# Linear attention of a decoder layer: values as the stationary operand, denominators in every lane

## The chip, the cores and the metric

The kernel runs on one core of a Trainium2 chip. The metric is the device time of the core in microseconds (us), taken over several executions; the median counts.

## The reference

One decoder layer in three parts, each followed by a layer norm over the sum with its input: causal linear attention with a feed-forward (the first layer), cross-attention to a context of 375 rows (the second), and a feed-forward with 8 experts (the third). Only the first layer's attention is touched:

```python
q = _phi((h @ wq).reshape(b, s, H, DH), proj)      # phi(x) = elu(x @ proj) + 1
k = _phi((h @ wk).reshape(b, s, H, DH), proj)
v = (h @ wv).reshape(b, s, H, DH)
# for each t, over the keys up to t:
kv = kv + k_t[..., :, None] * v_t[..., None, :]
ksum = ksum + k_t
num = einsum('bhd,bhde->bhe', q_t, kv)
den = einsum('bhd,bhd->bh', q_t, ksum) + 1e-06
out_t = num / den[..., None]
attn = out.reshape(b, s, H * DH) @ wo
```

There are 32 sequences of 112 rows, 256 columns wide, with H = 16 heads of DH = 64.

## The kernel before

The first layer works on 8 groups of 4 sequences: the first and the last are written out, the six between are a loop (`groups`, L222). All f32 weights and activations of the projections are split into a high and a low f16 part, and a product is three f16 products (`split_product`, L59). The scores and values of the attention are plain f32 products.

Inside a group the attention is worked in 16 units of four heads of one sequence (`unit`, L156); units 2n and 2n+1 are a pair, whose scores are computed together: even heads use array rows 0 to 63, odd heads rows 64 to 127. The order of the work is written out by hand: each engine has a `body(g)` that walks through 24 steps t, and issues what is due at that step. A unit passes these stations:

- `scores` (TensorE, L299): keys as weights, queries streamed, so that keys lie in the lanes: 112 keys x 112 queries per head, in one PSUM bank per half.
- `take_scores` (ScalarE, L439) copies the bank of a unit to one of four buffers `sm`; `mask` (GpSimd, L659) sets the entries above the diagonal to zero. Row 112 of `sm` holds 1e-6.
- `values` (TensorE, L312), two steps later: the scores of a head are the weights (112 columns), and 65 columns of `v1` are streamed, 64 of v and one of ones. Queries lie in the lanes of the result, and its 65th column is the denominator.
- `divide` (VectorE, L527), a step later: a reciprocal of 4 denominators per lane and a multiply of 256 columns into `o32`. Two PSUM banks `o_ps` alternate: values of unit u wait for the division of unit u-2.
- `turn_output` (TensorE, L321), once per pair: four turns through the identity bring the outputs to inner dimension in the lanes, in a bank of the shared pool `pb` of four.
- `out_high` (ScalarE, L429) and `out_low` (VectorE, L540) split the turned outputs into f16 parts.
- `rows_out` (TensorE, L328): the output projection with `wo`, once per sequence (four units), 24 products of 256 columns; it waits for the low halves.

Between these, the bodies place work of the neighbours: layer-norm statistics and rows of this group, the last and the next, the turn of the next group's normed rows (t = 15), its first two query tiles (t = 20), on VectorE the residual sums (L591). After the 24 steps come the rest of the next group's query, key and value projections, the turn of the second norm, the feed-forward with GELU, and its output rows; there `phi` (ScalarE L404, VectorE L518) and `take_v` (ScalarE, L421) follow TensorE. The pool `pb` is handed out in one fixed order of uses (`attention_uses`, L177; `MAIN`, L190), each waiting for the use four before.

Of the kernel before, what the change touches and what calls it, by code (L numbers as in the profile page):

```python
# [98 lines left out]
def layer1(nc, a, x_sb, ident, half_neg, consts_done, passed, sb_in, psum_in, sem):  # L99
# [7 lines left out]
    with stack:  # L107
# [24 lines left out]
        v1 = sb("v1", [P, G4, H, DH + 1], F32)  # L132
        sm = sb("sm", [P, NSM, 4 * T], F32)
        rec = sb("rec", [T, 2, 4], F32)
        o32 = sb("o32", [T, 2, 8 * DH], F32)
# [41 lines left out]
        def attention_uses(last):  # L177
            uses = []
            for t in range(STEPS):
                if TURN_AT <= t < UNITS + TURN_AT and (t - TURN_AT) % 2 == 1:  # L180
                    uses.append(("O", (t - TURN_AT) // 2))
                if t == T1_AT and not last:
                    uses += several("T1", KD)
                if t == Q_AT and not last:
                    uses += several("Q", EARLY)
                if t >= W_AT and (t - W_AT) % 4 == 0:
                    uses.append(("W", (t - W_AT) // 4))
            return uses
# [33 lines left out]
        def groups(eng, body):  # L222
# [13 lines left out]
        s_ready, s_copied, s_masked, av_done, rec_done, o_done, o_hi_done = (  # L236
            sem(f"a_{n}") for n in ("s_ready", "s_copied", "s_masked", "av_done", "rec_done", "o_done", "o_hi_done"))
# [16 lines left out]
        def _(pe):  # L254
# [57 lines left out]
            def values(g, u):  # L312
                b, heads = unit(u)
                pe.wait_ge(s_masked, UNITS * g + u + 1)
                at_least(pe, o_done, UNITS * g + u - 1)
                for i, h in enumerate(heads):
                    mm = pe.matmul(o_ps[u % 2][0:T, i * (DH + 1):(i + 1) * (DH + 1)], sm[0:T + 1, u % NSM, i * T:(i + 1) * T],
                                   v1[0:T + 1, b, h, :], start=True, stop=True)
                mm.then_inc(av_done, 1)

            def turn_output(g, j):  # L321
                pe.wait_ge(o_done, UNITS * g + 2 * j + 2)
                ps = claim(use(g, "O", j))
# [10 lines left out]
            def body(g):  # L334
                written(g, "V", 2 * G4)
                for t in range(STEPS):
# [4 lines left out]
                    if TURN_AT <= t < UNITS + TURN_AT and (t - TURN_AT) % 2 == 1:  # L341
                        turn_output(g, (t - TURN_AT) // 2)
# [43 lines left out]
        def _(act):  # L386
# [34 lines left out]
            def take_v(g, pieces):  # L421
                for i in pieces:
# [3 lines left out]
                    act.activation(v1[0:T, b, 8 * n:8 * n + 8, 0:DH], bank(u)[0:T, :].rearrange("p (h d) -> p h d", d=DH),  # L426
                                   ACT.Identity, scale=UNSCALE).then_inc(free_of(u), 1)

            def out_high(g, j):  # L429

                b, half = divmod(j, 2)
                u = use(g, "O", j)
                act.wait_ge(pb_ready, ready(u))
# [60 lines left out]
        def _(dve):  # L494
# [32 lines left out]
            def divide(g, u):  # L527

                ps = o_ps[u % 2][0:T, 0:4 * (DH + 1)].rearrange("p (i d) -> p i d", d=DH + 1)
                dve.wait_ge(av_done, UNITS * g + u + 1)  # L530
                at_least(dve, o_done, UNITS * g + u - 1)
                dve.reciprocal(rec[:, u % 2, :], ps[:, :, DH]).then_inc(rec_done, 1)
                dve.wait_ge(rec_done, UNITS * g + u + 1)
                if u >= 4:
                    dve.wait_ge(pb_ready, ready(use(g, "O", u // 2 - 2)))
                dst = o32[:, u // 2 % 2, :].rearrange("p (i r d) -> p r i d", r=2, d=DH)[:, u % 2, :, :]
                dve.tensor_tensor(dst, ps[:, :, 0:DH],
                                  rec[:, u % 2, :].unsqueeze(2).to_broadcast([T, 4, DH]), ALU.mult).then_inc(o_done, 1)

            def out_low(g, j):  # L540
                b, half = divmod(j, 2)
                u = use(g, "O", j)
# [109 lines left out]
        def _(pool):  # L652
# [28 lines left out]
            pool.memset(v1[:, :, :, 0:DH], 0.0).then_inc(pads_done, 1)  # L681
            pool.memset(v1[:, :, :, DH], 1.0).then_inc(pads_done, 1)
# [1379 lines left out]
```

## Time and profile before

| what | us |
|---|---|
| median of 3 runs | 2336.74 (2332.95 to 2337.68) |
| the profiled execution, its own time | 2328.24 |
| its span | 2326.5 |
| TensorE (PE) busy | 2204.5 (95%) |
| weight loads (PEld) busy, beside PE | 1646.4 (71%) |
| VectorE (DVE) busy | 1529.9 (66%) |
| ScalarE (ACT) busy | 1386.3 (60%) |
| GpSimd (POOL) busy | 763.1 (33%) |

The first layer fills the span up to about 750 us. A busy share is an average over stages. Matmul records overlap: one lasts longer than the step from its start to the next one's, so costs on TensorE are read from starts. An f32 product of scores or values stands as two records.

### The profile page before, as it was taken

What the parts mean: (1) busy time and instruction counts of PE and PEld (TensorE: products, weight loads), DVE (VectorE), ACT (ScalarE), POOL (GpSimd) and SP (SyncE); (2) the same over time, 40 slices, a digit from 0 to 9 for tenths busy, and PEclk for the clock granted to TensorE, in tenths of its full rate; (3) what the DMA queues carried; (4) which work ended last, traced back from release to release, by engine and by line L of the source; (5) the groups of instructions that cost most, each with busy time, mean ns of one, the idle gap of its engine ahead of it and who ended that gap; (6) DMA issues with size and microseconds to landing.
All of it is one profiled execution on the core that took longest, in us unless ns stands there. A gap on an engine that the chain in (4) does not pass through costs nothing. (4 is left out here: it accounts for less than half of the span.)

```text
span 2326.5 us, 57836 instructions
## 1 busy us (share of the span) xinstructions
PE 2204.5 (95%) x20778; PEld 1646.4 (71%) x20778; DVE 1529.9 (66%) x4387; ACT 1386.3 (60%) x3169; POOL 763.1 (33%) x1335
## 2 busy tenths in 40 slices
PE   5999999999997599999999999999999999989997
PEld 3776876876875366777677777767777767768886
DVE  4555455555544477777777777777777777566657
ACT  4556456456452367676767676776767676644534
POOL 1121221221211345444444444444445454200003
PEclk8999999999999699999999999999999999879999
DMA  5100000000000300000000000000000000042202
GB/s 137 39 2 1 0 0 0 0 0 0 0 1 1 102 10 16 10 16 11 15 14 12 16 10 15 10 16 10 16 10 15 10 9 2 1 109 91 92 1 64
DMA packets 45732, 51.44 MB, mean 22 GB/s; under 512 B 19120, under 2 KB 37664, under 8 KB 45504
## 3 DMA queue, kind: packets, MB, share of 16 engines
q1 hardware_dynamic: 45504, 48.45, 7.1%
q8 instruction: 137, 2.24, 0.4%
q14 instruction: 91, 0.75, 0.1%
HBM read 44.78 MB, written 3.67 MB: 21 GB/s over the span
## 5 line engine op out<-in xcount | busy, mean ns | idle before, releaser
L1450 POOL TENSOR_SCALAR p_norm<-p,p_rec 112x375 f32<-112x375 f32 x512 | 304.3, 596 | 630.5 <-DVE p_rec L1301 540.9
L1305 DVE TENSOR_TENSOR pt_lo<-b_t,pt_hi 125x336 f16<-125x336 f32 x512 | 258.0, 504 | 164.4 <-ACT pt_hi L1180 163.2
L1287 DVE CUSTOM_DVE_ANT_0 s_neg<-b_s,mask_bias 112x375 f32<-112x375 f32 x512 | 274.8, 537 | 95.6 <-PE b_s L1021 88.9
L1180 ACT ACTIVATE pt_hi<-b_t 125x336 f16<-125x336 f32 x512 | 227.6, 445 | 138.1 <-PE b_t L1030 136.2
L1174 ACT ACTIVATE p<-s_neg,neg_max 112x375 f32<-112x375 f32 x512 | 307.9, 601 | 0.5 <-DVE neg_max L1287 0.5
L1030 PE MATMUL b_t<-ident,p_norm 112*125 112x112 f32 x1536 | 274.2, 288 | 9.0 <-POOL p_norm L1450 2.5
L1030 PEld LDWEIGHTS b_t<-ident,p_norm 112*125 112x125 f32 x1536 | 215.6, 190 | 49.7 <-POOL p_norm L1450 26.9
L662 POOL TENSOR_SCALAR_AFFINE_SELECT sm<-sm 112x448 f32<-112x448 f32 x128 | 71.7, 584 | 424.8 <-ACT sm L442 424.8
L1154 ACT ACTIVATE v_hi<-b_pb 125x512 f16<-125x512 f32 x192 | 114.8, 598 | 109.9 <-PE b_pb L64 109.8
L62 PE MATMUL b_pb<-cn_hi,b_wk_hi 128*128 128x375 f16 x512 | 166.4, 325 | 2.1 <-DVE b_wk_lo L1332 2.1
L64 PE MATMUL b_pb<-cn_hi,b_wk_lo 128*128 128x375 f16 x512 | 165.6, 323 | 0.0
L63 PE MATMUL b_pb<-cn_lo,b_wk_hi 128*128 128x375 f16 x512 | 165.5, 323 | 0.0
L1151 ACT ACTIVATE k_hi<-b_pb 128x375 f16<-128x375 f32 x256 | 124.4, 486 | 61.4 <-PE b_pb L64 59.3
L442 ACT ACTIVATE sm<-a_s 112x448 f32<-112x448 f32 x128 | 62.6, 541 | 154.7 <-PE a_s L307 154.7
L62 PE MATMUL b_pb<-b_wv_hi,cn_hi 128*125 128x512 f16 x384 | 147.5, 384 | 5.2 <-issue 3.8
L64 PE MATMUL b_pb<-b_wv_hi,cn_lo 128*125 128x512 f16 x384 | 147.1, 383 | 0.0
L63 PE MATMUL b_pb<-b_wv_lo,cn_hi 128*125 128x512 f16 x384 | 147.0, 383 | 0.0
L1277 DVE SCALAR_TENSOR_TENSOR v_lo<-b_pb,v_hi 125x512 f16<-125x512 f32 x192 | 131.0, 682 | 18.2 <-ACT v_hi L1154 18.2
L1272 DVE SCALAR_TENSOR_TENSOR k_lo<-b_pb,k_hi 128x375 f16<-128x375 f32 x256 | 138.2, 540 | 1.7 <-ACT k_hi L1151 1.7
L1046 PE MATMUL b_o<-pt_hi,v_hi 125*64 125x112 f16 x1536 | 138.7, 222 | 0.0
L1046 PEld LDWEIGHTS b_o<-pt_hi,v_hi 125*64 125x64 f16 x1536 | 86.8, 110 | 71.4 <-issue 45.0
L1046 PE MATMUL b_o<-pt_hi,v_lo 125*64 125x112 f16 x1536 | 132.6, 214 | 0.0
(256 smaller groups left out, 6442.2 us busy)
## 6 DMA issues: line engine op xcount, KB each, us to landing
w_raw<-in_L_ffn_W_dram SPq DMA_DIRECT2D x16, 1024.0 KB, 7.5
ctx<-in_ctx_dram SPq DMA_DIRECT2D x32, 375.0 KB
out_dram<-c_z SPq DMA_DIRECT2D x8, 448.0 KB, 3.2
x_sb<-in_x_dram SPq DMA_DIRECT2D x1, 3136.0 KB, 19.1
ff<-in_L_attn_w_dram SPq DMA_DIRECT2D x2, 1024.0 KB, 6.4
y_t<-in_L_xattn_Wkv_dram SPq DMA_DIRECT2D x2, 1024.0 KB, 10.0
mask<-in_mask_BxS_bf_dram SPq DMA_DIRECT2D x32, 41.0 KB, 2.6
a_raw<-in_L_attn_wq_dram SPq DMA_DIRECT2D x1, 1024.0 KB, 5.0
```

Source lines behind the costliest of these rows:

```text
L62: pe.matmul(out, lh, rh, start=first, stop=False)
L63: pe.matmul(out, lh, rl, start=False, stop=False)
L64: return pe.matmul(out, ll, rh, start=False, stop=last)
L1030: mm = pe.transpose(t_ps[h % 2][0:JP, t * T:(t + 1) * T], p_norm[:, h % 4, t * JP:(t + 1) * JP], ident[0:T, 0:T])
L1046: mm = pe.matmul(o_ps[DH * r:DH * (r + 1), c:c + T], v2[:, par, t, (h + r) * DH:(h + r + 1) * DH], pt[:, (h + r) % 4, keys], start=(t == 0 ...
L1174: act.activation(p32[:, h % 4, :], s_neg[:, h % 2, :], ACT.Exp, bias=neg_max[:, h % 4:h % 4 + 1], scale=-1.0, accum_out=p_sum[:, h % 4:h % ...
L1180: act.activation(pt_hi[:, h % 4, :], t_ps[h % 2][0:JP, 0:JT * T], ACT.Identity).then_inc(pt_hi_done, 1)
L1272: ins = dve.scalar_tensor_tensor(k2_lo[:, par, j, 0:S2], ps[:, 0:S2], UNSCALE, k2_hi[:, par, j, 0:S2], ALU.mult, ALU.subtract)
L1277: ins = dve.scalar_tensor_tensor(v2_lo[:, par, t, cols], ps[0:JP, :], UNSCALE, v2_hi[:, par, t, cols], ALU.mult, ALU.subtract)
L1287: dve.tensor_tensor_reduce(s_neg[:, h % 2, :], s_ps[h % 2][0:T, 0:S2], mask_bias[:, par, :], -1.0, 3.4e38, ALU.add, ALU.min, neg_max[:, h ...
L1305: dve.tensor_tensor(pt_lo[:, h % 4, :], t_ps[h % 2][0:JP, 0:JT * T], pt_hi[:, h % 4, :], ALU.subtract).then_inc(pt_lo_done, 1)
L1450: pool.tensor_scalar(p_norm[:, h % 4, :], p32[:, h % 4, :], p_rec[:, h % 4:h % 4 + 1], 0.0, ALU.mult, ALU.add).then_inc(p_norm_done, 1)
```

## The change

Values become the weights and scores are streamed. A unit of `values` is now a step v of a pair: for two heads of each unit of the pair, 64 columns of v are the weights and the 112 score columns of the head are streamed. The head of the even unit writes to PSUM lanes 0 to 63, that of the odd unit to lanes 64 to 127. A new tile `ones` (64 columns of ones) as weights gives the denominators in the same lanes, in columns 224 to 447 of the bank. The outputs then have the inner dimension in the lanes already, so `turn_output`, its PSUM uses and its waits go. `divide` takes a reciprocal of 224 denominators in 128 lanes and multiplies 224 columns; `out_high` and `out_low` read `o32` in SBUF instead of a PSUM bank. Values of a pair's first step wait for the masks of both units, and copies of the scores for values of both units two pairs back. `v1` loses its column of ones.

```diff
-        v1 = sb("v1", [P, G4, H, DH + 1], F32)
+        v1 = sb("v1", [P, G4, INNER], F32)
+        ones = sb("ones", [P, DH], F32)
         sm = sb("sm", [P, NSM, 4 * T], F32)
-        rec = sb("rec", [T, 2, 4], F32)
-        o32 = sb("o32", [T, 2, 8 * DH], F32)
+        rec = sb("rec", [P, 2, 2 * T], F32)
+        o32 = sb("o32", [P, 2, 4, T], F32)
...
             for t in range(STEPS):
-                if TURN_AT <= t < UNITS + TURN_AT and (t - TURN_AT) % 2 == 1:
-                    uses.append(("O", (t - TURN_AT) // 2))
...
-            def values(g, u):
+            def values(g, v):
+
+                u = v - v % 2
                 b, heads = unit(u)
-                pe.wait_ge(s_masked, UNITS * g + u + 1)
-                at_least(pe, o_done, UNITS * g + u - 1)
-                for i, h in enumerate(heads):
-                    mm = pe.matmul(o_ps[u % 2][0:T, i * (DH + 1):(i + 1) * (DH + 1)], sm[0:T + 1, u % NSM, i * T:(i + 1) * T],
-                                   v1[0:T + 1, b, h, :], start=True, stop=True)
-                mm.then_inc(av_done, 1)
-
-            def turn_output(g, j):
-                pe.wait_ge(o_done, UNITS * g + 2 * j + 2)
-                ps = claim(use(g, "O", j))
-                for m in range(4):
-                    mm = pe.transpose(ps[:, m * T:(m + 1) * T], o32[:, j % 2, m * P:(m + 1) * P], ident[0:T, 0:T])
-                mm.then_inc(pb_ready, 1)
+                pe.wait_ge(s_masked, UNITS * g + u + 2)
+                at_least(pe, o_done, UNITS * g + v - 1)
+                ps = o_ps[v % 2]
+                for n in range(2):
+                    i = 2 * (v % 2) + n
+                    keys = slice(i * T, (i + 1) * T)
+                    for r in range(2):
+                        h = heads[i] + r
+                        pe.matmul(ps[DH * r:DH * (r + 1), n * T:(n + 1) * T], v1[0:T + 1, b, h * DH:(h + 1) * DH],
+                                  sm[0:T + 1, (u + r) % NSM, keys], start=True, stop=True)
+                for n in range(2):
+                    i = 2 * (v % 2) + n
+                    for r in range(2):
+                        mm = pe.matmul(ps[DH * r:DH * (r + 1), (2 + n) * T:(3 + n) * T], ones[0:T + 1, :],
+                                       sm[0:T + 1, (u + r) % NSM, i * T:(i + 1) * T], start=True, stop=True)
+                        if n == 1:
+                            mm.then_inc(av_done, 1)
...
-                        for u in (use(g, "O", 2 * b), use(g, "O", 2 * b + 1)):
-                            pe.wait_ge(free_of(u), freed(u))
+                        pe.wait_ge(o_lo_done, UNITS // 2 * g + 2 * b + 2)
...
-                act.activation(o_hi[:, b % 2, 4 * half:4 * half + 4, :], bank(u)[:, 0:4 * T].rearrange("p (m t) -> p m t", t=T),
-                               ACT.Identity).then_inc(o_hi_done, 1)
+                act.activation(o_hi[:, b % 2, 4 * half:4 * half + 4, :], o32[:, j % 2, :, :], ACT.Identity).then_inc(o_hi_done, 1)
...
-                at_least(act, av_done, UNITS * g + u + 1 - NSM)
+                at_least(act, av_done, 2 * (UNITS * g + u - u % 2 - 2))
...
-                dve.reciprocal(rec[:, u % 2, :], ps[:, :, DH]).then_inc(rec_done, 1)
+                dve.reciprocal(rec[:, u % 2, :], o_ps[u % 2][:, 2 * T:4 * T]).then_inc(rec_done, 1)
                 dve.wait_ge(rec_done, UNITS * g + u + 1)
-                if u >= 4:
-                    dve.wait_ge(pb_ready, ready(use(g, "O", u // 2 - 2)))
-                dst = o32[:, u // 2 % 2, :].rearrange("p (i r d) -> p r i d", r=2, d=DH)[:, u % 2, :, :]
-                dve.tensor_tensor(dst, ps[:, :, 0:DH],
-                                  rec[:, u % 2, :].unsqueeze(2).to_broadcast([T, 4, DH]), ALU.mult).then_inc(o_done, 1)
+                first = 2 * (u % 2)
+                dve.tensor_tensor(o32[:, u // 2 % 2, first:first + 2, :], o_ps[u % 2][:, 0:2 * T].rearrange("p (i t) -> p i t", t=T),
+                                  rec[:, u % 2, :].rearrange("p (i t) -> p i t", t=T), ALU.mult).then_inc(o_done, 1)
...
-                dve.tensor_tensor(o_lo[:, b % 2, 4 * half:4 * half + 4, :], bank(u)[:, 0:4 * T].rearrange("p (m t) -> p m t", t=T),
-                                  o_hi[:, b % 2, 4 * half:4 * half + 4, :], ALU.subtract).then_inc(free_of(u), 1)
+                dve.tensor_tensor(o_lo[:, b % 2, 4 * half:4 * half + 4, :], o32[:, j % 2, :, :],
+                                  o_hi[:, b % 2, 4 * half:4 * half + 4, :], ALU.subtract).then_inc(o_lo_done, 1)
...
-            pool.memset(v1[:, :, :, 0:DH], 0.0).then_inc(pads_done, 1)
-            pool.memset(v1[:, :, :, DH], 1.0).then_inc(pads_done, 1)
+            pool.memset(v1[:, :, :], 0.0).then_inc(pads_done, 1)
+            pool.memset(ones[:, :], 1.0).then_inc(pads_done, 1)
```

## Rows read from the trace of the kernel before

**Rows 1.** The page: busy time of each engine, share of the span, instructions
```profile
PE 2204.5 (95%) x20778; PEld 1646.4 (71%) x20778; DVE 1529.9 (66%) x4387; ACT 1386.3 (60%) x3169; POOL 763.1 (33%) x1335
```

**Rows 2.** By stretch: length, busy PE, PEld, DVE, ACT, POOL, PEclk, DMA share, GB/s
```profile
335.38:371.29 35.91, 35.91 (x375) 33.33 (x373) 23.23 (x72) 16.54 (x30) 10.36 (x18) 1.00 0.00 0
371.29:422.36 51.07, 49.28 (x319) 31.88 (x316) 22.58 (x48) 28.75 (x53) 7.12 (x6) 1.00 0.00 0
```

**Rows 3.** TensorE in order of time, two pairs of units: start, length, work
```profile
337.09 1.04 PE L307 MATMUL a_s<-qt,kt 64*112 64x112 f32 x16
338.06 1.79 PE L317 MATMUL a_o<-v,sm 113*112 113x65 f32 x16
339.69 0.55 PE L325 MATMUL a_pb<-ident,o 112*128 112x112 f32 x4
340.17 1.04 PE L307 MATMUL a_s<-qt,kt 64*112 64x112 f32 x16
```

**Rows 4.** The same view in the second layer: its values, column halves in f16
```profile
1502.63 0.22 PE L1046 MATMUL b_o<-pt_lo,v_hi 125*64 125x112 f16 x2
1502.68 0.21 PE L1046 MATMUL b_o<-pt_hi,v_lo 125*64 125x112 f16 x2
```

**Rows 5.** Busy time from first reciprocal to last low half: a middle, the last group
```profile
336.51:367.80 31.29, 31.29 (x335) 29.15 (x335) 22.24 (x70) 12.69 (x25) 10.15 (x18) 1.00 0.00 0
684.40:715.10 30.70, 29.36 (x320) 27.69 (x320) 18.35 (x55) 10.24 (x21) 8.82 (x16) 1.00 0.01 2
```

**Rows 6.** VectorE's groups by line in the middle one of these stretches
```profile
L537 DVE TENSOR_TENSOR o<-a_o,rec 112x256 f32<-112x256 f32 x16 | 6.8, 425 | 1.1
L544 DVE TENSOR_TENSOR o_lo<-a_pb,o_hi 128x448 f16<-128x448 f32 x8 | 5.0, 621 | 0.6 <-ACT o_hi L436 0.2
L532 DVE RECIPROCAL rec<-a_o 112x4 f32<-112x4 f32 x16 | 2.7, 171 | 3.7 <-PE a_o L317 3.7
```

**Rows 7.** Reciprocals of three widths, whole execution, groups by line
```profile
L1301 DVE RECIPROCAL p_rec<-p_sum 112x1 f32<-112x1 f32 x512 | 78.4, 153 | 0.0
L532 DVE RECIPROCAL rec<-a_o 112x4 f32<-112x4 f32 x128 | 22.1, 173 | 39.9 <-PE a_o L317 39.3
L1687 DVE RECIPROCAL r_rec<-r_sum 112x32 f32<-112x32 f32 x1 | 0.4, 353 | 0.0
```

**Rows 8.** Ordinary two-input operations of two widths, the same view
```profile
L1669 DVE TENSOR_TENSOR logits<-r_small,br 112x8 f32<-112x8 f32 x1 | 0.2, 167 | 2.1 <-PE r_small L1627 2.1
L1688 DVE TENSOR_TENSOR probs<-r_exp,r_rec 112x256 f32<-112x256 f32 x1 | 0.4, 424 | 0.0
```

**Rows 9.** The feed-forward's low half, all from SBUF, the same view
```profile
L620 DVE TENSOR_TENSOR ff<-neg_relu,ff 128x448 f16<-128x448 f32 x64 | 40.0, 625 | 2.2
```

**Rows 10.** GpSimd in order of time: the masks of one pair
```profile
338.99 1.12 POOL L662 TENSOR_SCALAR_AFFINE_SELECT sm<-sm 112x448 f32<-112x448 f32 x2 [1.57 <-ACT sm L442]
```

**Rows 11.** TensorE and VectorE in order of time: a projection, the stretch's end
```profile
345.84 0.55 PE L325 MATMUL a_pb<-ident,o 112*128 112x112 f32 x4
346.23 0.27 PE L62 MATMUL a_pb<-a_wo_hi,o_hi 128*112 128x256 f16 x1
...
348.94 0.35 PE L307 MATMUL a_s<-qt,kt 64*112 64x112 f32 x2
...
367.17 0.62 DVE L544 TENSOR_TENSOR o_lo<-a_pb,o_hi 128x448 f16<-128x448 f32 x1
...
368.67 0.27 PE L62 MATMUL a_pb<-a_wo_hi,o_hi 128*112 128x256 f16 x1
...
371.33 0.62 DVE L524 SCALAR_TENSOR_TENSOR qt<-a_pb,phi_exp 128x448 f32<-128x448 f32 x1 [3.53 <-ACT phi_exp L419]
```

**Rows 12.** Busy time by stretch in the second layer, columns as in rows 2
```profile
790.90:795.00 4.10, 3.23 (x38) 2.61 (x37) 1.24 (x2) 2.63 (x6) 0.50 (x1) 0.98 0.14 58
804.00:808.10 4.10, 2.32 (x19) 1.06 (x16) 2.19 (x7) 3.61 (x7) 0.00 (x0) 1.00 0.00 0
808.10:812.00 3.90, 1.96 (x6) 1.44 (x7) 1.61 (x8) 1.19 (x4) 1.17 (x2) 0.50 0.02 4
```

More of the change, by code:

```diff
@@ L235, in layer1 @@
         relu_done, exp_done = sem("a_relu_done"), sem("a_exp_done")
-        s_ready, s_copied, s_masked, av_done, rec_done, o_done, o_hi_done = (
-            sem(f"a_{n}") for n in ("s_ready", "s_copied", "s_masked", "av_done", "rec_done", "o_done", "o_hi_done"))
+        s_ready, s_copied, s_masked, av_done, rec_done, o_done, o_hi_done, o_lo_done = (
+            sem(f"a_{n}") for n in ("s_ready", "s_copied", "s_masked", "av_done", "rec_done", "o_done", "o_hi_done", "o_lo_done"))
         xs1_done, xs_done = sem("a_xs1_done"), sem("a_xs_done")
@@ L340, in body @@
                         values(g, t - VALUES_AT)
-                    if TURN_AT <= t < UNITS + TURN_AT and (t - TURN_AT) % 2 == 1:
-                        turn_output(g, (t - TURN_AT) // 2)
                     if t == T1_AT and not is_last(g):
@@ L425, in take_v @@
                     act.wait_ge(pb_ready, ready(u))
-                    act.activation(v1[0:T, b, 8 * n:8 * n + 8, 0:DH], bank(u)[0:T, :].rearrange("p (h d) -> p h d", d=DH),
-                                   ACT.Identity, scale=UNSCALE).then_inc(free_of(u), 1)
+                    act.activation(v1[0:T, b, n * 512:(n + 1) * 512], bank(u)[0:T, :], ACT.Identity,
+                                   scale=UNSCALE).then_inc(free_of(u), 1)
             def out_high(g, j):
                 b, half = divmod(j, 2)
-                u = use(g, "O", j)
-                act.wait_ge(pb_ready, ready(u))
+                act.wait_ge(o_done, UNITS * g + 2 * j + 2)
                 if half == 0 and b >= 2:
                     act.wait_ge(pb_ready, ready(use(g, "W", b - 2)))
-                act.activation(o_hi[:, b % 2, 4 * half:4 * half + 4, :], bank(u)[:, 0:4 * T].rearrange("p (m t) -> p m t", t=T),
-                               ACT.Identity).then_inc(o_hi_done, 1)
+                act.activation(o_hi[:, b % 2, 4 * half:4 * half + 4, :], o32[:, j % 2, :, :], ACT.Identity).then_inc(o_hi_done, 1)
             def take_scores(g, u):
                 act.wait_ge(s_ready, UNITS * g + u - u % 2 + 2)
-                at_least(act, av_done, UNITS * g + u + 1 - NSM)
+                at_least(act, av_done, 2 * (UNITS * g + u - u % 2 - 2))
                 act.activation(sm[0:T, u % NSM, :], s_ps[u % 2][0:T, 0:4 * T], ACT.Identity).then_inc(s_copied, 1)
@@ L527, in divide @@
             def divide(g, u):
-                ps = o_ps[u % 2][0:T, 0:4 * (DH + 1)].rearrange("p (i d) -> p i d", d=DH + 1)
-                dve.wait_ge(av_done, UNITS * g + u + 1)
+                dve.wait_ge(av_done, 2 * (UNITS * g + u + 1))
                 at_least(dve, o_done, UNITS * g + u - 1)
-                dve.reciprocal(rec[:, u % 2, :], ps[:, :, DH]).then_inc(rec_done, 1)
+                dve.reciprocal(rec[:, u % 2, :], o_ps[u % 2][:, 2 * T:4 * T]).then_inc(rec_done, 1)
                 dve.wait_ge(rec_done, UNITS * g + u + 1)
-                if u >= 4:
-                    dve.wait_ge(pb_ready, ready(use(g, "O", u // 2 - 2)))
-                dst = o32[:, u // 2 % 2, :].rearrange("p (i r d) -> p r i d", r=2, d=DH)[:, u % 2, :, :]
-                dve.tensor_tensor(dst, ps[:, :, 0:DH],
-                                  rec[:, u % 2, :].unsqueeze(2).to_broadcast([T, 4, DH]), ALU.mult).then_inc(o_done, 1)
+                first = 2 * (u % 2)
+                dve.tensor_tensor(o32[:, u // 2 % 2, first:first + 2, :], o_ps[u % 2][:, 0:2 * T].rearrange("p (i t) -> p i t", t=T),
+                                  rec[:, u % 2, :].rearrange("p (i t) -> p i t", t=T), ALU.mult).then_inc(o_done, 1)
             def out_low(g, j):
                 b, half = divmod(j, 2)
-                u = use(g, "O", j)
                 dve.wait_ge(o_hi_done, UNITS // 2 * g + j + 1)
-                dve.tensor_tensor(o_lo[:, b % 2, 4 * half:4 * half + 4, :], bank(u)[:, 0:4 * T].rearrange("p (m t) -> p m t", t=T),
-                                  o_hi[:, b % 2, 4 * half:4 * half + 4, :], ALU.subtract).then_inc(free_of(u), 1)
+                dve.tensor_tensor(o_lo[:, b % 2, 4 * half:4 * half + 4, :], o32[:, j % 2, :, :],
+                                  o_hi[:, b % 2, 4 * half:4 * half + 4, :], ALU.subtract).then_inc(o_lo_done, 1)
             def x_rows(g):
```

## The prediction

> **What bounds the kernel now.** I read the page first: TensorE is busy 95% of the span, VectorE 66% [rows 1]. A share is only an average, so I then cut the first layer's loop into the two halves of a group of four sequences. Its attention stretch, from the first values product to the third query projection, is 35.91 us with TensorE busy all of it and the clock granted in full (2.4 GHz), VectorE 23.23 us; the rest, to the next group's first values, is 51.07 us with TensorE busy 49.28 [rows 2], so a group takes 86.98 us. TensorE sets the pace in both, and VectorE has some 12 us to spare in the first.
>
> TensorE's order of time shows what a pair of units costs (a unit is four heads of one sequence): scores from 337.09 to 338.06 (0.97 us), values to 339.69 (1.63), the turn of the outputs to the next scores at 340.17 (0.48), 3.08 us in all [rows 3]. Eight pairs make 24.6 us of the 35.9. An f32 product stands as two records, so 16 records are the 8 products.
>
> **What the change does on TensorE.** It removes eight turns a group at 0.48 us, 3.85 us. Values were 16 records of 65 columns, 0.10 us apiece (1.63/16); they become 16 products of 112 columns, 32 records. The nearest f32 row of a product that shares the array is the scores': 16 records of 112 columns in two row halves, 0.97 us with a change of array shape in front. The other end is one record after another at 0.10 us. So 32 records cost some 1.6 us if column halves run together, 3.2 us if they don't. In f16 the trace shows that they do: the second layer's values, 112 columns, start two every 0.05 us [rows 4]. I take 1.6 us: values as dear as before, turns gone. New are changes of array shape between values and each output projection or early turn. The turns show the price of one: four of them to a projection in the same shape take 0.39 us (345.84 to 346.23), to the scores 0.48 [rows 3, 11], so 0.1 us; five a group are 0.5 us (bounds 0, and 0.2 each). TensorE's stretch would shrink by 3.4 us a group.
>
> **What it does on VectorE.** This term decides. From a group's first reciprocal to the end of its last low half of outputs are 31.29 us, VectorE busy 22.24 [rows 5], among it 16 reciprocals of 112x4 (2.7 us), 16 multiplies (6.8) and 8 low halves (5.0) [rows 6].
>
> The denominators now stand in every lane, one per head and query, so each reciprocal goes over 224 elements instead of 4. The trace has three widths: 1 element 153 ns, 4 elements 173, 32 elements 353 [rows 7]. That is 6.67 ns an element over the first interval and 6.43 over the second, while a TENSOR_TENSOR goes from 167 ns at 8 elements to 424 at 256, 1.04 ns each [rows 8]. From 32 elements on: 353 + 192 x 6.43 = 1588 ns. The bounds are far apart: 0.39 us if a wide one ran as an ordinary operation, and 2.47 us if the 353 ns were all per element (11.0 x 224). I take 1.59 since three widths lie on one line. The Trainium skill (VectorE: DVE Perf Modes, "First, the fixed hardware budget") says that the reciprocal is an iterated divide with a repeat count of 8, and gives VectorE 0.96 GHz; read as eight cycles an element, an estimate is 1.9 us, and the sum would end some 40 us higher. By the page's reading an element is a third dearer than the slope of the rows, and I keep the rows.
>
> Per group: 16 x (1.588 - 0.171) = +22.7 us; the multiply falls from 256 to 224 elements, 16 x 0.03 = -0.5. Low halves read SBUF instead of PSUM: 621 ns now, 625 for the same shape from SBUF [rows 6, 9], nothing. ScalarE's high halves and copies of v keep their sizes, and ScalarE is busy under half of the stretch (16.54 of 35.91 us): nothing. Values of an even unit now wait for both masks of the pair; these end at 340.11, the values behind the next scores start at 340.17 + 0.97 = 341.14 [rows 3, 10], and longer pairs make the slack greater: nothing. The copies' second wait asks for values of a pair earlier: nothing. The memsets before the loop keep their sizes, no DMA changes.
>
> VectorE's stream becomes 22.24 + 22.7 - 0.5 = 44.4 us, with 0.03 us between reciprocal and multiply 44.9. TensorE's is 31.3 - 3.4 = 27.9. So **VectorE becomes the bound of the attention stretch**, at 5.6 us a pair against TensorE's 2.6 (3.9 with a projection in every second pair). TensorE can't run ahead: a values product waits for the division two before it (two PSUM banks). Behind a projection it does 2.7 + 0.97 + 0.8 = 4.5 us (a projection before scores is 2.71 us, 346.23 to 348.94 [rows 11]) until the division has its values, while VectorE has two divisions of 1.95 and 1.6 to 2.2 us of low half, residual sum and norms, 5.5 to 6.1 us. The projections stay hidden.
>
> **The sum.** A middle group: 44.9 - 31.3 = +13.6 us at the last low half. Now the last projection starts 0.87 us behind that (367.80, 368.67) since two query tiles are in front [rows 11]; those will be done early, so 0.87 comes off, and 0.3 comes back because the fourth query tile then waits for VectorE's first query sum: that ends 4.15 us behind the last low half (371.33 + 0.62 - 367.80), and TensorE, behind the projection (2.7) and a tile (1.1), is there after 3.9. That is +13.0. I take the first group as a middle one; the last has VectorE busy 18.35 of 30.70 us [rows 5], so 18.35 + 22.7 = 41.1, +10.4. After the stretch TensorE is 96% busy: nothing is won back. Seven groups at 13.0 and one at 10.4 are +101 us. I add 1 us a group, +8, for a clock that falls at times. Against the profiled execution's 2328.24 us that is 2437; the median of the runs lies 8.5 us above that execution, so 2446 us.
>
> **The clock.** TensorE's busy share in the stretch falls to 50 to 70%. This trace has both outcomes for a TensorE that waits a good part of the time: it kept the clock where it was busy 3.23 of 4.1 us (granted 0.98, from 790.9), and where it was busy 2.32 of 4.1 us (from 804.0) it kept it to the end, then stood at 0.50, which is 1.2 GHz [rows 12]. The lightest part of a group, the pairs with layer norms, has 2.6 us and the pipeline's tails in 5.8. At 1.2 GHz a pair takes 5.2 us, still hidden.
>
> **Rivals.**
> 1. The wide reciprocal is cheap, and the change gains. At 0.39 us VectorE's stream is 22.24 + 16 x 0.22 - 0.5 = 25.3 us, under TensorE's 27.9, and the gain is 3.4 x 8 = 27 us: 2310 us. It decides while the reciprocal is under (27.9 - 22.24 + 2.7 + 0.5)/16 = 0.56 us; level with before is at 0.77 us. Three widths on a line stand against it. The Trainium skill (TensorEngine Tiling (Array Packing), "When to Use Tiling") recommends this swap for a free dimension of at most 64, and under "PSUM Bottleneck" warns that emptying PSUM may then bind; by my rows the warning holds. Chance 5%, and 2% for a price between that ends level.
> 2. f32 column halves run one after another: the shared use of the array isn't there. A pair is then 0.97 + 3.2 = 4.2 us on TensorE, still under 5.6; behind a projection 2.7 + 0.97 + 1.6 = 5.3 against 5.5 to 6.1. It would hardly show: 1.5 us a group more, 2458 us. For it: no f32 row has column halves. Chance 13%.
> 3. The clock falls in each group and stays low: behind a projection TensorE needs 9.0 us against 6.1 and 5.5, +2.9 and +3.5, the last projection +2.7, the dense work about 3 until it is back: up to 12 us a group. Half is likelier: +40, 2486 us. Chance 14%.
> 4. The reciprocal is dearer beyond 32 elements: eight ordinary element steps (8 x 1.04 = 8.3 ns) instead of 6.43, 353 + 192 x 8.3 = 1.95 us. That is 0.36 x 128 = +46, 2492 us. Against it: the slope holds from 1 to 32. The Trainium skill's repeat count of 8, on the page named above, would give this. Chance 6%.
>
> **The numbers.** The forecast has 60%; alone it ranges from 2430 to 2465 (switches, gaps and clock within 2 us a group). With cases 2 to 4, 2425 to 2495 leaves out some 2 in 10: the gain, the level case and the tails. A measurement of this kernel tells 0.2% (about 5 us) from no change: chances are 93% for slower by more than that, 2% for within it, 5% for faster by more.
>
> **What would show it.** Reciprocals of 128x224 at 1.59 us; VectorE busy over 95% of a stretch of 44 to 46 us; TensorE's values waiting for VectorE's division; scores of successive pairs 5 to 6.5 us apart; values' records two every 0.10 us; the rest of a group still near 51 us. Reciprocals under 0.8 us would sink the forecast, and so would divisions that wait for TensorE.

## The result, and the profile after

The changed kernel takes 2425.87 us (median of 4 runs, 2415.67 to 2433.7) beside 2336.66 for the kernel before on the same chip: ratio 1.038, 95% interval [1.034, 1.042]. It is slower, by 89 us; the forecast was 2446 us, 20 us too high. The profiled execution took 2426.17 us, its span 2424.5.

The page of after, busy time by engine and two of its groups:

```profile
PE 2218.6 (92%) x21546; PEld 1641.1 (68%) x21546; DVE 1690.6 (70%) x4387; ACT 1386.6 (57%) x3169; POOL 765.4 (32%) x1335
...
L531 DVE RECIPROCAL rec<-a_o 128x224 f32<-128x224 f32 x128 | 197.9, 1546 | 17.2 <-PE a_o L328 16.9
...
L323 PE MATMUL a_o<-sm,v 113*64 113x112 f32 x1024 | 80.6, 279 | 74.2 <-DVE o L534 73.6
```

Against [rows 1] VectorE has 161 us more; the reciprocals alone grew from 22.1 [rows 7] to 197.9. TensorE's idle time ahead of the values is 74.2 us where it was 0.2 in before, and nearly all of it is put down to the division. The waits of the first layer say it again, engine and line, what was waited for, total, times, longest:

```profile
ACT o_hi L437 <- DVE o L534: 95.0, 47, 4.8
PE a_o L323 <- DVE o L534: 73.6, 73, 1.9
```

By stretch, columns as in [rows 2]: the attention stretch and the rest of the same middle group, VectorE's stretch from first reciprocal to last low half as in [rows 5], then a stretch before and one in a fall of the clock:

```profile
373.47:421.49 48.02, 38.04 (x471) 32.81 (x469) 44.13 (x73) 16.54 (x30) 10.43 (x18) 0.93 0.00 0
421.49:472.56 51.07, 49.28 (x319) 31.88 (x316) 21.96 (x47) 28.73 (x52) 7.12 (x6) 1.00 0.00 0
374.62:418.77 44.15, 34.23 (x426) 29.00 (x421) 42.48 (x70) 14.11 (x28) 10.21 (x18) 0.92 0.00 0
386.00:389.90 3.90, 1.26 (x22) 1.08 (x24) 3.83 (x7) 1.19 (x3) 1.17 (x2) 1.00 0.00 0
389.90:393.30 3.40, 3.40 (x27) 3.12 (x23) 3.37 (x10) 0.19 (x1) 1.27 (x2) 0.50 0.00 0
```

The first stretch grew from 35.91 to 48.02 us; the second has the 51.07 us of before to the last digit. TensorE in order of time shows where the 12.1 us sit:

```profile
373.47 0.60 PE L323 MATMUL a_o<-sm,v 113*64 113x112 f32 x8
...
375.15 1.04 PE L306 MATMUL a_s<-qt,kt 64*112 64x112 f32 x16
376.65 0.60 PE L323 MATMUL a_o<-sm,v 113*64 113x112 f32 x8 [0.46 <-DVE o L534]
377.09 0.55 PE L328 MATMUL a_o<-sm,ones 113*64 113x112 f32 x8
378.96 0.60 PE L323 MATMUL a_o<-sm,v 113*64 113x112 f32 x8 [1.32 <-DVE o L534]
...
380.07 1.84 PE L306 MATMUL a_s<-qt,kt 64*112 64x112 f32 x16
```

The first pair, with both banks free, needs 1.68 us from values to scores (373.47 to 375.15), much as before (1.63 [rows 3]), and no turn follows. Of the group's other fourteen steps nine stand until VectorE has divided; four of the five that don't are right behind a projection, in which VectorE catches up. The scores of the next pair come 4.92 us behind; TensorE's clock stands at 1.2 GHz from 379.66 on, for 3.41 us, and they last 1.84 us. VectorE in order of time ends at the only wait that it has for TensorE in the stretch:

```profile
374.62 1.56 DVE L531 RECIPROCAL rec<-a_o 128x224 f32<-128x224 f32 x1
376.21 0.39 DVE L534 TENSOR_TENSOR o<-a_o,rec 128x224 f32<-128x224 f32 x1
376.52 0.42 DVE L496 BATCH_NORM_STATS2 a_stats<-xsum 112x6 f32<-112x256 f32 x1
...
395.48 0.42 DVE L587 SCALAR_TENSOR_TENSOR x<-a_pb,x_sb 112x256 f32<-112x256 f32 x1
396.95 1.56 DVE L531 RECIPROCAL rec<-a_o 128x224 f32<-128x224 f32 x1 [1.06 <-PE a_o L328]
```

**Where the time went.** From the first values to the next group's first values, the first layer's seven groups take 695.3 us against 609.2, the last 79.1 against 69.1: +96.1. The rest of the span, two layers that no kernel here changes, is 1575.5 us against 1574.1, +1.4. Over the fourteen traces of this case that rest goes from 1565.0 us (e4, the clock at 1.2 GHz for 58 us of it) to 1580.2 (e5, 94 us), so a few us of a total can't be given to the change.

### The profile page after: what moved, and what is told of

Read it like the earlier page. It is cut to its first block and busy times, and to the rows that moved or that the text cites. A ratio compares the mean times of both kernels' runs of the same rounds, so it can differ in the third digit from the quotient of the medians.

```text
span 2424.5 us, 59124 instructions
## 1 busy us (share of the span) xinstructions
PE 2218.6 (92%) x21546; PEld 1641.1 (68%) x21546; DVE 1690.6 (70%) x4387; ACT 1386.6 (57%) x3169; POOL 765.4 (32%) x1335
## 5 line engine op out<-in xcount | busy, mean ns | idle before, releaser
L531 DVE RECIPROCAL rec<-a_o 128x224 f32<-128x224 f32 x128 | 197.9, 1546 | 17.2 <-PE a_o L328 16.9
L323 PE MATMUL a_o<-sm,v 113*64 113x112 f32 x1024 | 80.6, 279 | 74.2 <-DVE o L534 73.6
```

What stands on the lines that cost most here:

```text
L531: dve.reciprocal(rec[:, u % 2, :], o_ps[u % 2][:, 2 * T:4 * T]).then_inc(rec_done, 1)
```

## The experiments

"Group" below is the mean of seven from first values to first values, in the profiled execution: 87.0 us before, 99.3 after. Ratios are against the kernel before on the same chip.

### Is it the reciprocal, and is it the only thing?

**e1_cheap**: the changed kernel with an ordinary operation in the reciprocal's place; the division is left out.

```diff
-                dve.reciprocal(rec[:, u % 2, :], o_ps[u % 2][:, 2 * T:4 * T]).then_inc(rec_done, 1)
+                dve.tensor_scalar(rec[:, u % 2, :], o_ps[u % 2][:, 2 * T:4 * T], 0.0, 1e-6, ALU.mult, ALU.add).then_inc(rec_done, 1)
```

> The changed kernel with its reciprocal of 224 elements replaced by an ordinary VectorE operation of the same shape and source (den x 0 + 1e-6); the division itself is left out, everything else of the change stays. My theory (the reciprocal's length is the whole loss): VectorE's stream per group falls from 44.2 to about 25 us, below TensorE's 28, TensorE is the bound again and the turns it no longer makes are a gain: 2336.7 - 27 = about 2310 us (2300 to 2320). Rival (new array shapes, the wait for both masks, the SBUF sources or the longer TensorE work cost the time): it stays above 2400 us.

Measured: 2312.6 us, ratio 0.989 [0.985, 0.993], group 85.2. Its page and its TensorE in order of time:

```profile
L531 DVE TENSOR_SCALAR rec<-a_o 128x224 f32<-128x224 f32 x128 | 48.7, 381 | 32.2 <-PE a_o L328 31.8
```

```profile
330.83 1.04 PE L306 MATMUL a_s<-qt,kt 64*112 64x112 f32 x16
331.80 0.60 PE L323 MATMUL a_o<-sm,v 113*64 113x112 f32 x8
332.23 0.55 PE L328 MATMUL a_o<-sm,ones 113*64 113x112 f32 x8
...
333.48 1.04 PE L306 MATMUL a_s<-qt,kt 64*112 64x112 f32 x16
```

With the per-element price gone, all of the loss is gone and a gain is left. A pair is 2.65 us from scores to scores (330.83 to 333.48) where before it was 3.08 [rows 3]: the turn really is saved. But a group gains 1.8 us, not 3.4. In the group shown in [rows 2], before's eight turns sum to 3.4 us. About 0.8 us of that go to changes of array shape (values to a projection 0.48 to 0.51 where the turn had 0.39, the early turn of the normed rows to values 0.92 instead of 0.77, a projection 2.76 instead of 2.71), and about 0.8 us to waits in the part with the first projection.

**e2_before_wide**: the kernel before, with a reciprocal of 224 elements added per unit, whose result nothing reads.

```diff
...
+                dve.reciprocal(wide[:, u % 2, :], o_ps[u % 2][0:T, 0:224])
                 dve.reciprocal(rec[:, u % 2, :], ps[:, :, DH]).then_inc(rec_done, 1)
```

> The kernel before, turns and all, with one more reciprocal per unit, of 112x224 elements from PSUM into a tile that nobody reads. My theory: VectorE's stream per group is 22.2 + 16 x 1.55 = 47 us against 31.3, so each group grows by some 15 us and the kernel by 115 to 120 us, to about 2453 us, a little slower than the changed kernel (2426), because it keeps the small reciprocals. Rival (the loss comes with the swapped operands on TensorE): under 2360 us, since VectorE has 9 us of idle time in the stretch to take part of it.

Measured: 2450.21 us, ratio 1.049 [1.044, 1.055], group 102.7. Its groups of VectorE:

```profile
L533 DVE RECIPROCAL wide<-a_o 112x224 f32<-112x224 f32 x128 | 197.8, 1546 | 20.8 <-PE a_o L318 20.6
...
L534 DVE RECIPROCAL rec<-a_o 112x4 f32<-112x4 f32 x128 | 15.3, 120 | 0.0
```

The price alone, put into the untouched kernel, makes it as slow as the change does and more: 15.7 us a group against 12.3 in after. Of the 3.4 between them the small reciprocals (16 x 0.12) and the wider multiply (425 ns against 392) are 2.4. The rest is open; the clock differs too, at 1.2 GHz for 130 us of the first layer where after has 61 (both without the first 60 us of the kernel).

**e4_w96**: the changed kernel, the reciprocal over 96 of the 224 columns (`WIDE` is 96); the division of the others is left out.

```diff
-                dve.reciprocal(rec[:, u % 2, :], o_ps[u % 2][:, 2 * T:4 * T]).then_inc(rec_done, 1)
+                dve.reciprocal(rec[:, u % 2, 0:WIDE], o_ps[u % 2][:, 2 * T:2 * T + WIDE]).then_inc(rec_done, 1)
...
```

> The changed kernel with the reciprocal over the first 96 of the 224 columns only; the others keep 1e-6, so their division is left out. By the slope of 6.2 ns it takes 353 + 64 x 6.2 = 750 ns, close to the 770 ns at which I put the break-even: VectorE's stream 22.24 - 2.7 - 0.5 + 16 x 0.78 = 31.5 us against 31.3 before, less the 0.87 us that the last projection waited for: 2330 us (2322 to 2342), no difference that can be told from before. Rival (a threshold other than VectorE's stream decides): above 2350 or below 2315 us.

Measured: 2333.72 us (10 runs), ratio 1.000 [0.998, 1.002]. The row of the reciprocal, and under it VectorE's stretch, columns as in [rows 2]:

```profile
L532 DVE RECIPROCAL rec<-a_o 128x96 f32<-128x96 f32 x128 | 95.4, 746 | 27.1 <-PE a_o L329 26.9
```

```profile
340.40:373.65 33.25, 30.34 (x425) 26.12 (x422) 30.39 (x70) 13.12 (x26) 10.96 (x18) 1.00 0.00 0
```

By its medians this is the break-even of the prediction (0.77 us). By its groups, 88.6 us against 87.0, it lies past it: a straight line from e1 (0.38 us, 85.2) to e4 (0.75 us, 88.6) meets 87.0 at 0.57 us. From e4 down at the slope that e4 and after give, 13.4 us of group per us of reciprocal, it is 0.62 us. Both are estimates. In the profiled execution the first layer is 12.6 us longer than in before, and the unchanged rest 9.1 us shorter (1565.0 against 1574.1); why it is shorter no run shows. In the stretch shown neither engine is busy throughout, VectorE 30.4 and TensorE 30.3 of 33.25 us: TensorE stands 2.9 us for divisions, and VectorE 2.3 us behind two projections. Near the break-even the two wait for one another in turn, and no sum of one engine's work is the length. The widths 1, 4, 32, 96 and 224 take 153, 173, 353, 746 and 1546 ns, 6.1 to 6.7 ns an element between neighbours.

### Do f32 column halves share the array?

**e3_cheap_blocked**: e1 with the loops over halves and heads exchanged, for values and for ones, so that products of one lane half stand together in the queue.

```diff
-                for n in range(2):
-                    for r in range(2):
+                for r in range(2):
+                    for n in range(2):
...
```

> e1 with the order of the small products changed: the two products for lanes 0 to 63 first, then the two for lanes 64 to 127, in place of turns by halves. If column halves run together only when neighbours in the queue use different halves, the middle of each block goes one after the other: of 8 products of a step some 2 in 8 still overlap, and a pair costs 2.4 to 3.2 us for values instead of 1.6. TensorE is the bound without the long reciprocal, so 0.8 to 1.6 us x 64 pairs = 50 to 100 us over e1, 2360 to 2410 us. Rival (the array takes the halves from a queue of their own, or they never overlapped and 1.6 us has another cause): the same as e1 within 5 us.

Measured: 2316.93 us, ratio 0.990 [0.985, 0.995], group 85.6; the theory's 2360 and more was wrong, its rival (as e1 within 5 us) right. TensorE in order of time:

```profile
331.43 0.61 PE L322 MATMUL a_o<-sm,v 113*64 113x112 f32 x8
331.87 0.60 PE L327 MATMUL a_o<-sm,ones 113*64 113x112 f32 x8
...
333.17 1.04 PE L306 MATMUL a_s<-qt,kt 64*112 64x112 f32 x16
```

Eight records still take 0.38 to 0.44 us. The halves overlap whichever way the queue is ordered within these eight records; only the end of a pair is 0.05 us later.

**e5_serial**: the changed kernel, all products of values and ones into lanes 0 to 63 (so nothing can share), division on 64 lanes; the odd heads and lanes 64 to 127 are left out.

```diff
-                        pe.matmul(ps[DH * r:DH * (r + 1), n * T:(n + 1) * T], v1[0:T + 1, b, h * DH:(h + 1) * DH],
+                        pe.matmul(ps[0:DH, n * T:(n + 1) * T], v1[0:T + 1, b, h * DH:(h + 1) * DH],
...
```

> The changed kernel, reciprocals as they are, with all the small products of values and denominators sent to lanes 0 to 63, so that no two of them can share the array; reciprocal and multiply read those lanes only, and what the odd heads and lanes 64 to 127 would have held is left out. My theory (rival 2 of the prediction: with VectorE as the bound it would hardly show): values of a pair take 3.1 us or more instead of 1.7, a pair 4.1 against VectorE's 5.5; only behind a projection (2.8 + 1.0 + 1.6 = 5.3 us) it comes close: 0 to 2 us a group, 2426 to 2440 us. Rival (TensorE's longer work is part of the 89 us): +1.4 us a pair, 64 pairs, up to 2515 us.

Measured: 2441.12 us, ratio 1.045 [1.041, 1.050]. TensorE in order of time:

```profile
376.54 1.04 PE L306 MATMUL a_s<-qt,kt 64*112 64x112 f32 x16
377.51 0.98 PE L323 MATMUL a_o<-sm,v 113*64 113x112 f32 x8
378.33 0.93 PE L328 MATMUL a_o<-sm,ones 113*64 113x112 f32 x8
...
380.72 1.04 PE L306 MATMUL a_s<-qt,kt 64*112 64x112 f32 x16
```

Values of a pair take 3.21 us (377.51 to 380.72) instead of 1.68, and yet the kernel is only 15 us over after: VectorE's division of 64 lanes still costs 1.54 us and covers most of it. What shows is behind two projections, where VectorE now waits 2.4 us a group for TensorE (1.06 in after). The price of the prediction's second rival was right, its premise was not.

**e6_cheap_serial**: e5 with e1's ordinary operation.

```diff
-                dve.reciprocal(rec[0:DH, u % 2, :], o_ps[u % 2][0:DH, 2 * T:4 * T]).then_inc(rec_done, 1)
+                dve.tensor_scalar(rec[0:DH, u % 2, :], o_ps[u % 2][0:DH, 2 * T:4 * T], 0.0, 1e-6, ALU.mult, ALU.add).then_inc(rec_done, 1)
```

> The same, all products in lanes 0 to 63, on e1, whose reciprocal is an ordinary operation (no division). Here TensorE is the bound, so the lost sharing must show in full: 16 more steps of 0.096 us a pair = 1.5 us, 64 pairs, +98 us over e1: 2410 us (2395 to 2425). If products of column halves gained nothing by running together, it would stay at e1's 2313.

Measured: 2406.28 us, ratio 1.031 [1.027, 1.036]. With VectorE out of the way, the same serial products cost 94 us over e1 (2406.3 - 2312.6), 64 pairs at 1.5 us; by groups 96.6 against 85.2 us, 1.4 a pair. Sharing by column halves is what makes the new form level with the old on TensorE.

### Can the inverse come from elsewhere?

In e7 to e12 nothing of the computation is left out. The inverse is ScalarE's function 1/sqrt, squared by a second pass, in place of VectorE's reciprocal; its precision is that of ScalarE's table.

**e7_act_root**: this for 12 of a group's 16 units, behind the copies of the next scores; VectorE then waits for `inv_done` in place of its reciprocal.

```diff
...
+                act.activation(root_rec[:, u % 2, :], o_ps[u % 2][:, 2 * T:4 * T], ACT.Abs_reciprocal_sqrt).then_inc(root_done, 1)
+                act.wait_ge(root_done, k + 1)
+                act.activation(rec[:, u % 2, :], root_rec[:, u % 2, :], ACT.Square).then_inc(inv_done, 1)
...
```

> The changed kernel with 12 of 16 reciprocals a group taken from VectorE: ScalarE computes 1/sqrt(den) and squares it, two passes over 128x224; every fourth unit keeps VectorE's reciprocal. Nothing is left out, but 1/den has the precision of ScalarE's table. VectorE's stream: 19.0 + 4 x 1.58 = 25.4 us, ScalarE 16.5 + 12 x 0.8 = 26 us, TensorE 29.5 (31.3 less the 1.8 that e1 gained): TensorE is the bound again, about as e1: 2313 us (2305 to 2328), faster than before. Rival (ScalarE's chain of two passes and its place in front of the high halves makes a new wait): 2335 us or more. One more table load a group on ScalarE, 1.3 us, should be hidden.

Measured: 2375.18 us, ratio 1.016 [1.011, 1.021], group 92.7: 60 us over the theory, in the rival's range. ScalarE in order of time:

```profile
370.93 0.98 ACT L462 ACTIVATE sm<-a_s 112x448 f32<-112x448 f32 x2 [4.31 <-PE a_s L316]
371.79 0.36 ACT L455 ACTIVATE root_rec<-a_o 128x224 f32<-128x224 f32 x1
372.18 0.39 ACT L457 ACTIVATE rec<-root_rec 128x224 f32<-128x224 f32 x1
```

ScalarE stood for 4.31 us in front of a copy of scores, with the ones' products of the unit long done (366.46 + 0.58 us on TensorE); the inversion queued behind that copy, and the products after those scores waited for the inversion.

**e8_act_newton**: all 16 on ScalarE, same order, and a Newton step of two VectorE operations.

```diff
...
+                dve.tensor_tensor(newton[:, u % 2, 0, :], o_ps[u % 2][:, 2 * T:4 * T], rec[:, u % 2, :], ALU.mult).then_inc(rec_done, 1)
+                dve.wait_ge(rec_done, UNITS * g + u + 1)
+                dve.scalar_tensor_tensor(newton[:, u % 2, 1, :], newton[:, u % 2, 0, :], 2.0, rec[:, u % 2, :], ALU.subtract,
+                                         ALU.mult).then_inc(newton_done, 1)
...
```

> All 16 reciprocals of a group from ScalarE as 1/sqrt squared, with one Newton step on VectorE (two more operations of 224 elements per unit), which restores f32 precision; nothing is left out. VectorE 19.0 + 16 x 0.65 = 29.4 us, ScalarE 16.5 + 16 x 0.8 = 29.3, TensorE 29.5: three engines level, so every wait between them shows. 2325 to 2350 us, most likely 2335, no gain. Rival (each is under TensorE, the waits overlap): 2313 us as e7. Other rival (the chain values, root, square, three operations in a row no longer fits two PSUM banks): above 2380 us.

Measured: 2516.56 us, ratio 1.078 [1.072, 1.083], the slowest of all, as its other rival had it (above 2380). From its waits between 60 and 840 us, in the first layer:

```profile
DVE newton L556 <- ACT rec L458: 160.7, 52, 10.5
PE a_o L334 <- DVE o L562: 95.1, 54, 2.5
```

Each engine waits for the next: the chain of ScalarE's two passes (355 and 390 ns in e7) and VectorE's three (385, 414 and 391 ns), behind the same queue order as in e7, no longer fits behind two PSUM banks. The order's share is not told apart, since no run has the Newton step with the early order. TensorE's clock stood at 1.2 GHz for 181 us of the first layer, against 10 in before (without the first 60 us).

**e9_act_early**: e7 with the inversion ahead of the copies.

```diff
+                    if 3 <= t < UNITS + 3:
+                        invert(g, t - 3)
                     if t < UNITS and t % 2 == 0 and t > 0:
                         take_scores(g, t)
                         take_scores(g, t + 1)
-                    if 3 <= t < UNITS + 3:
-                        invert(g, t - 3)
```

> e7 with one change of order: on ScalarE the inversion of a unit stands ahead of the copies of the next pair's scores instead of behind them (the copies wait for scores that TensorE issues only after the next products with the values, and the inversion is what the products after those wait for). Nothing is left out; 12 of a group's 16 inverses still come from ScalarE's table of 1/sqrt, squared. Theory (e7 lost its time to this order, not to the three-engine chain as such): from the end of the ones' products the chain is 0.36 + 0.39 us on ScalarE and 0.39 on VectorE with some 0.1 at each handover, 1.4 us, while TensorE has the other unit's values and a pair of scores, 1.8 us, in between, so it is covered; the four units with VectorE's own reciprocal take 1.55 + 0.39 + 0.1 = 2.0 us, 0.25 over, 1 us a group. Group 85.2 + 1 = 86.2 us, total 2312.6 + 8 = 2321, range 2312 to 2330: below before (2336) by 0.3 to 1.0%. Rival (the handovers over three engines cost it whatever the order): it stays at e7's 2375, with ScalarE's out rounding copies now waiting for VectorE instead.

Measured: 2350.6 us, ratio 1.009 [1.006, 1.012], group 89.4. The order was worth 25 us (3.3 us a group), but the total lies 20 us above the theory's range, and the kernel is still slower than before.

**e10_act_all** and **e11_act_half**: e9 with 16 and with 8 of 16 inverses on ScalarE. The edit is e10's; e11 has `u % 2 == 0` there.

```diff
         def on_act(u):
-            return u % 4 != 3
+            return u >= 0
...
```

> e9 with all 16 inverses of a group on ScalarE (no Newton step, nothing left out). Theory 1: VectorE then has only the 0.39 us multiply in the chain for every unit, so the 0.25 us of each fourth unit goes: group 85.2 to 85.5 us, total 2313 to 2316. Theory 2: ScalarE binds in pairs that follow one another with no projection between: two copies 0.98, four passes 1.50, one rounding copy 0.56 = 3.04 us against TensorE's 2.66; in a group some 4 pairs are of that kind, 0.4 us each, +1.5 us a group: total 2325. VectorE's part in the wait falls to nothing in both; the page's line of TensorE's waits then names ScalarE's copies of scores.

> e9 with 8 of 16 inverses on ScalarE, the other 8 (every second unit) as VectorE's reciprocal. VectorE per pair 1.55 + 2 x 0.39 = 2.33 us plus the low half of 0.62 = 2.95 us against TensorE's 2.66 with no projection between; with its other work in the first part (18 us of 31 in before, of which products and low halves are most) it is about level. Theory: 8 units with 0.25 to 0.3 us over the cover, 2 to 2.5 us a group over e1: 87.5 us, total 2331, level with before. Rival (VectorE's stream binds in the first part as in after, at half the excess): group 90 to 92 us, total 2350 to 2370.

Measured: e10 2337.17 us, ratio 1.002 [1.001, 1.004], group 87.1; e11 2385.28 us, ratio 1.022 [1.020, 1.025], group 93.1. So four reciprocals that stay on VectorE cost 2.3 us a group (e9 less e10), and eight cost 5.9: more than twice what I expected of each (0.25 us a unit), and e11 came out behind even its rival's range. The price is not spread evenly. Both TensorE waits that make it up in e9 are seen in its trace:

```profile
351.39 0.60 PE L333 MATMUL a_o<-sm,v 113*64 113x112 f32 x8 [0.99 <-DVE o L560]
...
378.36 0.32 PE L62 MATMUL a_pb<-a_wo_hi,o_hi 128*112 128x256 f16 x1 [1.27 <-DVE o_lo L566]
```

The first stands for the division of the fourth unit and comes 0.92 us later behind the step before it than in e10 (1.98 us against 1.05). The second is the last projection, which waits for the low half behind the sixteenth unit's division, 1.43 us later (3.70 us behind the query tiles' start against 2.27). The eighth and twelfth unit have a projection behind them and cost nothing. So a long reciprocal is paid for in full where no projection covers it.

e10 was above both its theories; ScalarE in order of time, and under it TensorE:

```profile
336.78 0.98 ACT L462 ACTIVATE sm<-a_s 112x448 f32<-112x448 f32 x2 [2.75 <-PE a_s L316]
337.78 1.28 ACT L455 ACT_TABLE_LOAD   x1
339.07 0.36 ACT L455 ACTIVATE root_rec<-a_o 128x224 f32<-128x224 f32 x1
```

```profile
338.24 1.04 PE L316 MATMUL a_s<-qt,kt 64*112 64x112 f32 x16
340.49 0.60 PE L333 MATMUL a_o<-sm,v 113*64 113x112 f32 x8 [1.21 <-DVE o L560]
```

The first inversion of a group brings a table load of 1.28 us, since GELU comes before it, and TensorE waits 1.21 us for that.

**e12_act_warm**: e10 with a tiny activation of the same kind while ScalarE waits for the first scores.

```diff
                     take_v(g + 1, range(V_EARLY, 2 * G4))
+                    act.activation(warm[:, 0:1], g1[:, 0:1], ACT.Abs_reciprocal_sqrt)
                     for u in range(2):
                         take_scores(g + 1, u)
```

> e10 with one tiny activation of the 1/sqrt kind (128 x 1, its result unread) on ScalarE behind the last copy of values of a group and ahead of the first copies of scores. In e10's trace ScalarE loads a function table for 1.28 us at the first inversion of each group (eight of these loads, each 1.28 us), and TensorE's third unit of values then comes 2.25 us behind its scores where the other pairs need 0.97: 1.28 us a group. Ahead of the first scores ScalarE is idle for 8.35 us, so the load is hidden there. Theory: group 87.1 - 1.3 = 85.8 us, 7 groups -9, total 2337 - 9 = 2328 (2320 to 2332), 0.2 to 0.5% below before. Rival (the wait moves to the next pair, whose chain over ScalarE is 0.13 to 0.3 us over its cover already, or the table is loaded again at the copies): 2334 to 2338, as e10.

Measured, as its theory had it: 2324.56 us (12 runs, 2314.45 to 2329.2), ratio 0.995 [0.993, 0.997], group 86.0. The first group still pays for its load; the seven others don't. ScalarE in order of time:

```profile
320.99 1.28 ACT L497 ACT_TABLE_LOAD   x1
322.28 0.20 ACT L497 ACTIVATE warm<-a_g 128x1 f32<-128x1 f32 x1
329.32 0.98 ACT L463 ACTIVATE sm<-a_s 112x448 f32<-112x448 f32 x2 [6.84 <-PE a_s L317]
```

The load now lies in an idle stretch, and the activation follows it after 0.01 us. This version beats both kernels, if narrowly: about 4% below after, 0.5% below before, and 0.6% above e1, which has no inverse at all. e10 and e12 ran on different chips, so their ratios (1.002 and 0.995) and groups (87.1 and 86.0) are compared, not the times.

## Why the prediction was right, and where a size was off

**The bound moves to VectorE: right.** Busy 42.48 of 44.15 us, 96%, where over 95% of 44 to 46 us was expected. e1 takes the loss away by the reciprocal's price alone, e2 brings it by that alone.

**The price of the reciprocal: right within 3%.** 1546 ns against 1588: the line through the three small widths of [rows 7] held up to seven times the largest of them. The nearly free end, 0.39 us, was that of an ordinary operation (381 ns in e1) and did not apply; neither did the fourth rival's 1.95. The Trainium skill (VectorE: DVE Perf Modes, "First, the fixed hardware budget") has the repeat count of 8 from which I had estimated 1.9 us; the measured 6.2 ns an element stands against reading it as eight cycles of 0.96 GHz, 8.3 ns.

**The sum of a group: 14.0 us forecast with the clock, 12.1 measured in the group shown.** The stretch that I put at 44.9 us came out at 44.15 with a wait of 1.06 in it, which I had kept apart. Two terms were too large. The reciprocals, 16 x (1.588 - 1.545), took 0.7 less. And I had added durations to a busy time: in a dense stream a record starts some 0.08 us before the one ahead ends (376.21 + 0.39 is 376.60, the next starts at 376.52), so that the durations of VectorE's records exceed its busy time by 4.0 us in after's stretch against 3.0 in before's, 1.1 more for as many records. The 0.3 us for the fourth query tile did not appear as such either: the last projection starts 0.05 us behind the last low half, and the rest is the 51.07 us of before. The last group cost 10.0 us against 10.4. The even step was wrong, too: I had expected scores of successive pairs 5 to 6.5 us apart. In the group shown they are 4.92, 4.56, 10.29, 2.65 and 7.73 us apart, 6.0 in the mean, since behind a projection VectorE has caught up and TensorE runs two steps without a wait.

**TensorE's gain: 1.8 us a group instead of 3.4**, by e1. Values of 1.6 us a pair and the vanished turn were right (1.68, and 0.43 a pair). The sum took each of the eight turns at 0.48 us, 3.85 in all, though [rows 11] has 0.39 for one ahead of a projection; in the group of [rows 2] only three are at 0.48 and five at 0.38 to 0.39, 3.4 in all. That is 0.5 us of the miss. Too small were the shape changes, about 0.8 us for 0.5, and I had no term for the waits of a chain that comes close to its cover, 0.8 us. Since VectorE bound the stretch, none of it showed in the time.

**The clock: right in size, by a smaller mechanism than the third rival's.** In the group shown it falls to 1.2 GHz twice, for 3.41 us each (from 379.66 and from 389.90), the second time behind a part in which TensorE is busy 1.26 of 3.9 us (386.0 to 389.9). Without the first 60 us, that makes 61 us in the first layer against 10 before. It does not stay low. The second fall meets a projection, which takes 3.79 us (391.13 to 394.92) instead of 2.76, and VectorE waits 1.06 us. The first costs nothing that shows: the group from 274.37 has only the second and takes 99.1 us as well. I had allowed 1 us a group without such a chain behind it, so that the size agrees is luck. In e5 the serial products keep TensorE busier, the clock is low for 14 us only, and the same projection takes 2.76 us. So e5's 15 us over after are net of about 1 us a group that after loses to the clock.

**The offset: wrong.** I had added 8.5 us since before's median lay that far over its profiled execution. After's median lies at its profiled execution. Of the miss of 20 us, 8.5 are this and some 13 the group terms above (109.4 forecast in the first layer, 96.5 measured with the 0.4 ahead of the first values); the unchanged layers took 1.4 more and so made the miss smaller. Nearly every error made the forecast too high; it is the reciprocals' 22 us a group, 16 x (1.545 - 0.171), that carried it.

**The break-even: 0.77 us forecast.** Medians of e4 agree (0.75 us, ratio 1.000), its groups put it at about 0.6. I had let VectorE's stream alone decide. In e4 that stream is short enough, 30.4 us busy against 31.3 of before's stretch, but the stretch takes 33.25: waits of each engine for the other, which the sum had at nothing, are the difference.

## What to carry to other kernels

When an operand swap removes a transpose, ask what the swap multiplies: here one denominator per query and head became one per lane of the head, 56 times as many elements an instruction, for an operation that costs 6 times an ordinary one per element. Price such an operation from two or three widths that the trace already has, and hold the engine's stream, not its share of the span, against the bound. That works where one engine is clearly the longer; near the break-even look at each step and what covers it, as e4 and e9 show. If the new form is wanted still, the place of the operation in the second engine's queue, how many stay behind and where its table is loaded decide whether moving it pays: these three alone lead from 1.6% above before (e7) to 0.5% below it (e12).

## What was not expected of the hardware

- Records of two f32 products into different column halves start together, a pair every 0.096 us (16 pairs of records in 1.68 us with the shape change), in either order of the eight records that was tried (e1, e3). All in one half, a single record starts every 0.10 us (e5).
- A reciprocal of 224 elements per lane costs the same on 128 lanes (1546 ns), 112 (1546, e2) and 64 (1537, e5).
- The reciprocal of 4 elements takes 173 ns in before and 120 ns right behind another one (e2).
- A change of ScalarE's function table cost the load and no more in both traces shown: 1.28 us, with the next activation 0.01 us behind (e12) and TensorE 1.21 us late (e10). The Trainium skill (ScalarE: Activation LUTs, "What ACT_TABLE_LOAD costs") gives 1283 ns for the load, as here, and adds 1380 ns of drain, which neither run shows.
